# Sums over fields of x2 as three f32r matmuls in place of one fp32 matmul, on one core

## The reference

```python
x0 = xk = e                       # (512, 39, 16): rows, fields, depth
outs = []
for W in (f0, f1, f2):            # f0: (39*39, 128), f1 and f2: (39*128, 128)
    z = einsum('bfd,bgd->bfgd', x0, xk).reshape(b, f * g, d)
    cur = einsum('bpd,pm->bmd', z, W)
    outs.append(cur)
    xk = cur
z = sum(concatenate(outs, axis=1), axis=-1)          # over the depth d
h = maximum(concatenate([z, dense_ctx], axis=1) @ W_top1 + b_top1, 0)
h = maximum(h @ W_top2 + b_top2, 0)
y = h @ W_top3
```

## Time and profile before

| | |
|---|---|
| three runs, median | 807.4 us (805.65 to 807.54) |
| profiled execution | 809.94 us, span 808.1 us |
| TensorE matmul busy | 698.5 us, 86% |
| VectorE busy | 621.5 us, 77% |
| ScalarE busy | 488.2 us, 60% |
| GpSimd busy | 256.1 us, 32% |

### The profile page before, as it was taken

One profiled execution on the slowest core, in us unless ns is written; L12 is line 12 of the kernel. 1 busy time (PEld: TensorE's weight loads), 2 busy tenths in 40 slices (PEclk: granted clock), 3 DMA queues, 4 the chain that ended last, 5 costly groups with the idle time before them and its releaser, 6 DMA issues.

```text
span 808.1 us, 12253 instructions
## 1 busy us (share of the span) xinstructions
PE 698.5 (86%) x3327; PEld 498.2 (62%) x3327; DVE 621.5 (77%) x1409; ACT 488.2 (60%) x1659; POOL 256.1 (32%) x247
## 2 busy tenths in 40 slices
PE   0107899999999999999999979999999998999977
PEld 0002556666667776666666766666666686767757
DVE  1004698999999885799899865799899986799960
ACT  0002566776778663776677644676678564768851
POOL 6750026432661240812741330622651000211110
PEclk9999799999999999999999999999999999999989
DMA  3710202120212020020302020020202010020000
GB/s 82 282 41 1 72 10 61 25 70 13 66 22 72 10 64 22 5 80 2 85 4 80 2 66 21 4 75 8 77 12 72 9 57 25 3 78 1 2 0 1
DMA packets 23423, 33.96 MB, mean 42 GB/s; under 512 B 7816, under 2 KB 10616, under 8 KB 22967
## 3 DMA queue, kind: packets, MB, share of 16 engines
q1 hardware_dynamic: 18230, 31.84, 12.8%
q0 software_dynamic: 5120, 1.29, 1.9%
HBM read 9.13 MB, written 0.00 MB: 11 GB/s over the span
## 4 chain that ended last, share of the span: by engine, by line
PE 49%; DVE 25%; issue 11%; another core or an unknown queue 8%; ACT 5%; DVEq 1%; DMA 0%; SPq 0%; ACTq 0%
DVE sums L621 12%; PE x_ps L738 10%; PE v_ps L713 5%; PE v_ps L715 5%; PE v_ps L714 5%; PE s_ps L766 4%; PE a_ps L713 4%; PE a_ps L714 4%; PE a_ps L715 4%; DVE z_sb L594 3%; ACT scaled L419 3%; DVE scaled L564 2%; DVE sums L569 2%; PE s_ps L845 2%
## 5 line engine op out<-in xcount | busy, mean ns | idle before, releaser
L419 ACT ACTIVATE scaled<-a_ps,x0c 128x128 f32<-128x128 f32 x1216 | 352.2, 385 | 211.1 <-PE a_ps L715 187.6
L621 DVE SCALAR_TENSOR_TENSOR sums<-v_ps,x0c,sums 128x128 f32<-128x128 f32 x768 | 215.4, 341 | 59.2 <-PE v_ps L715 54.6
L363 POOL DMA_INDIRECT e_sb<-in_tables,ids_now x140 | 166.5, 1189 | 40.3 <-issue 38.1
L713 PE MATMUL v_ps<-w_hi,x_hi 128*128 128x512 f32 x320 | 175.8, 549 | 4.0 <-DVE w_lo L537 2.0
L379 POOL TENSOR_TENSOR diag_sb<-x0c,eye_sb 128x320 f32<-128x320 f32 x64 | 63.2, 988 | 360.3 <-PE s_ps L845 357.2
L738 PE MATMUL x_ps<-z_sb,w_sb 117*128 117x512 f32 (+1 forms) x210 | 115.0, 629 | 20.4 <-DVE z_sb L594 18.8
L715 PE MATMUL v_ps<-w_hi,x_lo 128*128 128x512 f32 x320 | 127.6, 399 | 0.0
L714 PE MATMUL v_ps<-w_lo,x_hi 128*128 128x512 f32 x320 | 127.5, 399 | 0.0
L713 PE MATMUL a_ps<-w_hi,x_hi 128*128 128x512 f32 (+1 forms) x320 | 124.4, 389 | 0.6 <-issue 0.5
L714 PE MATMUL a_ps<-w_lo,x_hi 128*128 128x512 f32 (+1 forms) x320 | 123.5, 386 | 0.0
L715 PE MATMUL a_ps<-w_hi,x_lo 128*128 128x512 f32 (+1 forms) x320 | 123.2, 385 | 0.0
(11 more groups left out here) (77 smaller groups left out, 659.4 us busy)
## 6 DMA issues: line engine op xcount, KB each, us to landing
b_sb<-a_sb SPq DMA_DIRECT2D x300, 78.0 KB
w_sb<-in_w SPq DMA_DIRECT2D x1, 2496.0 KB
e_sb<-in_tables,ids_now POOLq DMA_INDIRECT x140
s_sb<-in_w SPq DMA_DIRECT2D x2, 1024.0 KB
wt_sb<-in_wt SPq DMA_DIRECT2D x1, 768.0 KB
s_sb<-in_w SPq DMA_DIRECT2D x1, 512.0 KB
wt_sb<-in_wt SPq DMA_DIRECT2D x1, 512.0 KB
w_raw<-in_w0a SPq DMA_DIRECT2D x1, 409.5 KB
```

What stands on the lines that cost most here:

```text
L363: pool.indirect_dma_start(out=e_sb[0:rows, i, :], out_offset=None, in_=tables, in_offset=bass.IndirectOffsetOnAxis(ap=ids_now[0:rows, 0, i ...
L419: last = nc.scalar.activation(scaled[:, s % 2, to, j, :], bank[:, j * MAPS:(j + 1) * MAPS], ACT.Copy, scale=x0c[:, k % 4, s, lo + j:lo + j ...
L621: nc.vector.scalar_tensor_tensor(out=sums[:, s % 2, j, :], in0=v_ps[n % 2][:, j * MAPS:(j + 1) * MAPS], scalar=x0c[:, k % 4, s, lo + j:lo ...
L713: nc.tensor.matmul(to, high, w_high, start=True, stop=False)
```

## The change

S of a tile becomes three f32r matmuls: x2 high times diagonal high, x2 high times diagonal low, x2 low times diagonal high. The parts are made so:

- ScalarE rounds `x0c` to `x0c_hi`, once a chunk at step 18, and `x2t` to `x2_hi`, once a tile: tile 0 at step 11, tile 1 at step 16, tile 2 at step 1 of the next slot, tile 3 at step 6 of the next slot.
- GpSimd subtracts to get `x0c_lo`, once a chunk, and `x2_lo`, once a tile. It spreads both parts of x0, so a tile has two spreads in place of one.
- TensorE waits for `x2_lo_ready` where it waited for `x2t_ready`, and for two spreads in place of one.
- `z_first`, used at the start only, becomes a view of `scaled`, which makes room in SBUF.

VectorE's program keeps its instructions; one of its waits names `x2_lo_ready` in place of `s_done`.

```diff
--- before.py
+++ after.py
@@ -65,6 +65,12 @@
 
 
 S_AT = ((1, 4, 6, 9), (10, 12, 14, 17), (2, 6, 11, 17), (2, 6, 11, 17))
+
+
+X0C_HI_AT = 18
+
+
+X2_HI_AT = (11, 16, HALVES + 1, HALVES + 6)
 
 SPLIT_AT = (5, 8, 10, 13)
 X0_TURN_AT = (15, 17)
@@ -149,16 +155,23 @@
         a_sb = sb("a_sb", [3 * F0, COLS])
         b_sb = sb("b_sb", [3 * F0, SHIFT_BUFS, COLS])
         z0_sb = sb("z0_sb", [3 * F0, 2, COLS])
-        z_first = sb("z_first", [3 * F0, T0, COLS])
         w0_raw = sb("w0_raw", [3 * F0, 2, T0, MAPS])
         x1_hi = sb("x1_hi", [128, 2, COLS], f32r)
         x1_lo = sb("x1_lo", [128, 2, COLS], f32r)
 
         scaled = sb("scaled", [128, 2, SCALED, 4, MAPS])
         sums = sb("sums", [128, 2, 4, MAPS])
+
+        z_first = scaled.rearrange("p a g f m -> p (a g f m)")[0:3 * F0, 0:T0 * COLS]\
+            .rearrange("p (i c) -> p i c", c=COLS)
         pace = sb("pace", [128, 1, FH], i32)
         x2t = sb("x2t", [128, 2, SUBS, MAPS])
-        diag_sb = sb("diag_sb", [128, 2, SB, F0 + 1])
+        x2_hi = sb("x2_hi", [128, 2, SUBS, MAPS], f32r)
+        x2_lo = sb("x2_lo", [128, 2, SUBS, MAPS], f32r)
+        x0c_hi = sb("x0c_hi", [128, 2, SUBS, F0 + 1], f32r)
+        x0c_lo = sb("x0c_lo", [128, 2, SUBS, F0 + 1], f32r)
+        diag_hi = sb("diag_hi", [128, 2, SB, F0 + 1], f32r)
+        diag_lo = sb("diag_lo", [128, 2, SB, F0 + 1], f32r)
 
         s_sb = sb("s_sb", [128, 4 * FG, BT])
         out0 = sb("out0", [128, B])
@@ -221,6 +234,10 @@
         tail_step = sem("tail_step")
         x2t_ready = sem("x2t_ready")
 
+        x2_hi_ready = sem("x2_hi_ready")
+        x2_lo_ready = sem("x2_lo_ready")
+        x0c_hi_ready = sem("x0c_hi_ready")
+        x0c_lo_ready = sem("x0c_lo_ready")
         diag_ready = sem("diag_ready")
         s_done = sem("s_done")
         s_ready = sem("s_ready")
@@ -372,15 +389,31 @@
                     if h in diag_at and exists(t, k - 1):
                         s = diag_at.index(h)
                         before = tile_of(t, k - 1, s)
-                        pool.wait_ge(x0c_ready, 4 * t + k)
+                        if s == 0:
+                            pool.wait_ge(x0c_hi_ready, 4 * t + k)
+                            if not isinstance(t, int) or 4 * t + k - 1 >= 2:
+
+                                pool.wait_ge(diag_ready, 2 * tile_of(t, k - 2, 0))
+                            nc.gpsimd.tensor_tensor(x0c_lo[:, (k - 1) % 2, :, :], x0c[:, (k - 1) % 4, :, :],
+                                                    x0c_hi[:, (k - 1) % 2, :, :].bitcast(fp32),
+                                                    ALU.subtract).then_inc(x0c_lo_ready, 1)
                         if not isinstance(t, int) or before >= 2:
 
                             pool.wait_ge(s_done, before - 1)
+                        spread = mask.rearrange("p (b a) -> p b a", a=1).broadcast_to([128, SB, F0 + 1])
                         nc.gpsimd.tensor_tensor(
-                            diag_sb[:, s % 2, :, :],
-                            x0c[:, (k - 1) % 4, s:s + 1, :].broadcast_to([128, SB, F0 + 1]),
-                            mask.rearrange("p (b a) -> p b a", a=1).broadcast_to([128, SB, F0 + 1]),
-                            ALU.mult).then_inc(diag_ready, 1)
+                            diag_hi[:, s % 2, :, :],
+                            x0c_hi[:, (k - 1) % 2, s:s + 1, :].bitcast(fp32).broadcast_to([128, SB, F0 + 1]),
+                            spread, ALU.mult).then_inc(diag_ready, 1)
+                        pool.wait_ge(x0c_lo_ready, 4 * t + k)
+                        nc.gpsimd.tensor_tensor(
+                            diag_lo[:, s % 2, :, :],
+                            x0c_lo[:, (k - 1) % 2, s:s + 1, :].bitcast(fp32).broadcast_to([128, SB, F0 + 1]),
+                            spread, ALU.mult).then_inc(diag_ready, 1)
+                        pool.wait_ge(x2_hi_ready, before + 1)
+                        nc.gpsimd.tensor_tensor(x2_lo[:, (k - 1) % 2, s, :], x2t[:, (k - 1) % 2, s, :],
+                                                x2_hi[:, (k - 1) % 2, s, :].bitcast(fp32),
+                                                ALU.subtract).then_inc(x2_lo_ready, 1)
                     if k % 2 == 1 and h == GATHER_AT + 1 and exists(t, k + 3):
 
                         nc.gpsimd.tensor_tensor(pace[:, :, :], table_rows_sb[:, :, :], table_rows_sb[:, :, :],
@@ -435,11 +468,27 @@
                         act.wait_ge(x0c_done, 4 * t + k + 2)
                         if not isinstance(t, int) or 4 * t + k + 1 >= 4:
 
-                            act.wait_ge(diag_ready, tile_of(t, k - 2, 0))
+                            act.wait_ge(x0c_lo_ready, 4 * t + k - 2)
                             act.wait_ge(x2t_ready, tile_of(t, k - 2, 0))
                         nc.scalar.activation(x0c[:, (k + 1) % 4, :, 0:F0],
                                              turn_ps[:, 0:SUBS * F0].rearrange("p (s f) -> p s f", s=SUBS),
                                              ACT.Copy).then_inc(x0c_ready, 1)
+                    if h == X0C_HI_AT and exists(t, k):
+                        if not isinstance(t, int) or 4 * t + k >= 2:
+
+                            act.wait_ge(diag_ready, 2 * tile_of(t, k - 1, 0))
+                        nc.scalar.activation(x0c_hi[:, k % 2, :, :], x0c[:, k % 4, :, :],
+                                             ACT.Copy).then_inc(x0c_hi_ready, 1)
+                    for s in range(SUBS):
+                        of = k if X2_HI_AT[s] < HALVES else k - 1
+                        if h == X2_HI_AT[s] % HALVES and exists(t, of):
+                            before = tile_of(t, of, s)
+                            act.wait_ge(x2t_ready, before + 1)
+                            if not isinstance(t, int) or before >= 2 * SUBS:
+
+                                act.wait_ge(s_done, before - 2 * SUBS + 1)
+                            nc.scalar.activation(x2_hi[:, of % 2, s, :], x2t[:, of % 2, s, :],
+                                                 ACT.Copy).then_inc(x2_hi_ready, 1)
                     if h == X1_HI_AT and exists(t, k + 1):
                         act.wait_ge(x1_step, T0 * (4 * t + k + 2))
                         nc.scalar.activation(x1_hi[:, (k + 1) % 2, :], x1_ps[:, :], ACT.Copy).then_inc(x1_hi_ready, 1)
@@ -574,7 +623,7 @@
                     dve.wait_ge(tail_step, TAIL * tile + 5)
                     if not isinstance(t, int) or 4 * t + k >= 2:
 
-                        dve.wait_ge(s_done, tile - 2 * SUBS + 1)
+                        dve.wait_ge(x2_lo_ready, tile - 2 * SUBS + 1)
                     nc.vector.tensor_tensor(x2t[:, k % 2, s, :], acc[:, 0, :], acc[:, 1, :],
                                             ALU.add).then_inc(x2t_ready, 1)
 
@@ -838,13 +887,17 @@
                         if s == 0 and tile is not None and k == 1:
 
                             pe.wait_ge(out2_ready, tile + 1)
-                        pe.wait_ge(diag_ready, before + 1)
-                        pe.wait_ge(x2t_ready, before + 1)
+                        pe.wait_ge(diag_ready, 2 * before + 2)
+                        pe.wait_ge(x2_lo_ready, before + 1)
                         if not isinstance(t, int) or before > 0:
                             pe.wait_ge(s_ready, before)
-                        nc.tensor.matmul(s_ps[:, 0:SB * (F0 + 1)], x2t[:, (k - 1) % 2, s, :],
-                                         diag_sb[:, s % 2, :, :].rearrange("p b f -> p (b f)"),
-                                         start=True, stop=True).then_inc(s_done, 1)
+                        to = s_ps[:, 0:SB * (F0 + 1)]
+                        x0_high = diag_hi[:, s % 2, :, :].rearrange("p b f -> p (b f)")
+                        nc.tensor.matmul(to, x2_hi[:, (k - 1) % 2, s, :], x0_high, start=True, stop=False)
+                        nc.tensor.matmul(to, x2_hi[:, (k - 1) % 2, s, :],
+                                         diag_lo[:, s % 2, :, :].rearrange("p b f -> p (b f)"), start=False, stop=False)
+                        nc.tensor.matmul(to, x2_lo[:, (k - 1) % 2, s, :], x0_high,
+                                         start=False, stop=True).then_inc(s_done, 1)
 
             def first_pairs():
```

## The result

The changed kernel takes 839.3 us (median of four runs, 833.3 to 842.0), the kernel before, measured beside it, 806.9 us (805.7 to 807.5). The ratio is 1.039, with a 95% interval of 1.034 to 1.045: 32 us slower. The forecast was 819.0 us with a range of 803 to 833. Its direction was right, and its size was off by 20 us. Where the runs of a kernel spread, its ratio rests on those within 1.5% of its fastest. The profiled execution was the fastest of the four, 833.3 us, so that the profile holds 23.3 us of the loss (span 831.4 against 808.1 us).

The account below looks back on a forecast made before the run. VectorE was taken to bound ordinary slots, TensorE the dense ones. Terms -2.8 (TensorE), +9.5 (GpSimd on VectorE), +2.5 (ScalarE) and +2.4 (end) sum to +11.6 us on 807.4, so 819.0 us, range 803 to 833.

Parts of the forecast that it names:

- What bounds the kernel: VectorE sets the pace in the twelve ordinary slots, TensorE in the three slots where dense layers run.
- TensorE, -2.8 us: S matmuls: three f32r replace one fp32, saving 0.10 us a tile; 1.2 us in dense slots, 1.6 us in ordinary ones.
- What GpSimd does to VectorE, +9.5 us: Ordinary slots: GpSimd's added SBUF reads delay VectorE's two-SBUF-input operations; 7.9 us by rate, taken as 9.5 us.
- my upper bound of 25: Ordinary slots: each new GpSimd run costs VectorE one more full delay of 0.53 us, 48 tiles, 25 us.
- GpSimd's own added time: GpSimd: one more spread and a subtraction a tile, one subtraction a chunk; 111 us added in all.
- the rate of 0.095 us for each microsecond of spreads: VectorE delay per microsecond of GpSimd spreads, from L564 and L569; 10.5 us on 111 us, three quarters counted: 7.9 us.
- The bound of 0.53 us for each run: Upper bound for VectorE: each new GpSimd run costs one full delay as at 410.67, 25 us over 48 tiles.
- ScalarE, +2.5 us: Added roundings of x0c_hi and x2_hi, 24.3 us of work mostly hidden in waits; 1.8 plus 0.7 us reach the time.
- the term's two places: x0c_hi ahead of the a_sb copy, 1.8 us; x2_hi of tile 0 ahead of a dense layer's activations, 0.7 us.
- The end, +2.4 us: After the last x2t: longer chain +1.2 us, shorter matmuls -0.4 us; three more VectorE delays there, +1.6 us.
- every run of GpSimd costing a full operation: Rival: each GpSimd run costs VectorE 0.53 us a tile in ordinary slots, 25.4 us, time 834.9 us; chance 0.10.

Follow-up runs that it names:

- e8: Kernel before, with the fp32 S matmul made three f32r matmuls of the same two operands, nothing added on ScalarE or GpSimd: 802.3 us, ratio 0.995.
- e1: Kernel before, with a second spread and subtractions added on GpSimd alone, written to a spare buffer: 830.2 us, ratio 1.032.
- e14: Kernel before, with a second spread of the same size directly behind each spread, into a tensor nobody reads: 817.6 us, ratio 1.015.
- e9: Kernel before, with ScalarE's added roundings alone, at the steps of the change, into tensors nobody reads: 808.8 us, ratio 1.005.
- e13: Changed kernel with x0c_hi rounded at step 5 in place of 18, nothing else moved: 830.4 us, ratio 1.032 to the kernel before.
- e7: Changed kernel unaltered, measured again: 841.0 us, ratio 1.044 to the kernel before.

## Why the prediction was wrong

**What bounds the kernel.** Right. VectorE sets the pace of the ordinary slots, and what it lost there came out as time. The copy of x0c, once a chunk, before and after:

```profile
L440 ACT ACTIVATE x0c<-turn_ps x16: 316/320/332, 74.3 to 734.2; 128x156 f32<-128x156 f32 x16
```

```profile
L473 ACT ACTIVATE x0c<-turn_ps x16: 318/319/332, 74.7 to 755.0; 128x156 f32<-128x156 f32 x16
```

Between the first and the last lie 659.9 us before and 680.3 after, 20.4 of the 23.3 us. By the starts of the single copies, the twelve ordinary intervals grew by 2.2 us each, where I had said 0.5 to 1, and the three with dense layers, which I had said would not grow, fell by 2.1 us each; a boundary between two intervals may have moved too.

**TensorE, -2.8 us.** Right in mechanism and close in size: -4.0 us (e8). The step of 0.44 us is there. TensorE's timeline after:

```profile
338.45 0.31 PE L896 MATMUL s_ps<-diag_hi,x_hi 128*128 128x320 f32 x1
338.60 0.30 PE L897 MATMUL s_ps<-diag_lo,x_hi 128*128 128x320 f32 x1
338.74 0.31 PE L899 MATMUL s_ps<-diag_hi,x_lo 128*128 128x320 f32 x1
338.89 1.02 PE L787 MATMUL x_ps<-z_sb,w_sb 117*128 117x512 f32 x2
```

**What GpSimd does to VectorE, +9.5 us.** This is the step that failed: 25.7 us for it alone (e1, 20.5 to 30.7), 16 us more than I took, and at my upper bound of 25. It was the mis-sized term of a mechanism that is there. The means of L564 and L569 rose as foretold, to 785 and 739 ns, and VectorE's busy time by three times the 10 us that I named. GpSimd's own added time was close (97.5 us, 111 predicted). Two parts of the step were wrong.

First, the rate of 0.095 us for each microsecond of spreads. I read it from two lines and let the others "only add". All lines together had 10.5 us of delays for 63.2 us of spreads, 0.166; on 111 us, at three quarters, that is 13.8 us where mine gave 7.9. After the change z0 (13.3 us) and the 128x896 addition (6.9 us), which my rate left out, carry nearly half of the 43.4 us, and TensorE waits for z0.

Second, that rate came from a trace in which a spread nearly always stands alone, and I applied it to operations in a row. A lone spread delays VectorE's next operation by what is left of the spread, and can start beside the multiply-adds; the second and third of a row start when VectorE is past these. I wrote that two in a row make the second likelier to be in the way, and then added 1.6 us for it: e14 shows 12 us for the second alone. The count shows what the row adds. Waits through one operation grew about as GpSimd's operations did (23 to 72, where those went from 79 to 223), from 9.6 to 24.8 us. Waits through two to five are new, 15.7 us on ten operations, in e1 13.1 us on eleven. The bound of 0.53 us for each run had no place for them, since it took it that VectorE waits through no more than one. Mostly that holds; z0 at 258.54 lost 2.88 us at once. Why those ten were not let in, the runs do not tell.

**ScalarE, +2.5 us.** 4.3 us (e9, 2.0 to 6.5), over the term. Of it 1.0 us lies behind the last x2t, which the forecast has under the end: in e9's trace the 39 matmuls start 3.4 us after x2t, before 2.4. The 3.3 us left are within the bounds of the term's two places (3.6 and 1.2 us). x0c_hi is likely a good part of it: its move gave back 10 us in the changed kernel (e13 against e7), though there x0c_lo moves with it.

**The end, +2.4 us.** 3.7 us: from VectorE's last four multiply-adds to the 39 matmuls it is 9.47 us before (from 774.03) and 13.17 after (from 795.78). Of this 1.6 us lie ahead of the last x2t, as forecast for VectorE's delays there, and 2.1 behind it, where I had 0.8 (+1.2 and -0.4). The last x2t, and what follows it, after:

```profile
803.78 0.69 DVE L627 TENSOR_TENSOR x2t<-sums 128x128 f32<-128x128 f32 x1
804.29 0.50 POOL L414 TENSOR_TENSOR x_lo<-x2t,x_hi 128x128 fp32r<-128x128 f32 x1
804.51 0.31 ACT L490 ACTIVATE x_hi<-x2t 128x128 fp32r<-128x128 f32 x1 [0.18 <-DVE x2t L627]
...
804.89 0.60 PE L896 MATMUL s_ps<-diag_hi,x_hi 128*128 128x320 f32 x1 [1.31 <-POOL x_lo L414]
...
806.12 0.45 POOL L414 TENSOR_TENSOR x_lo<-x2t,x_hi 128x128 fp32r<-128x128 f32 x1
...
806.92 0.61 PE L896 MATMUL s_ps<-diag_hi,x_hi 128*128 128x320 f32 x1 [0.89 <-ACT s_sb L464]
...
808.95 0.77 PE L815 MATMUL s_ps<-s_sb,w_sb 128*128 128x128 f32 x2 [0.89 <-ACT s_sb L464]
```

The third copy of S releases the last matmuls, as I had said, but not because it stands behind x2_hi. It is late because the third S matmul (804.89) waited 1.31 us for x2_lo of its tile (804.29): from 795.75 to 806.57 GpSimd works without a break, and in the end it is GpSimd that sets the pace. I had counted it there beside VectorE and for the last x2_lo only. That the total came near the term, and within its bounds of 0 and 5, is partly luck.

**The sum.** The single runs give 25.7 + 4.3 - 4.0 = 26.0 us, and 27.1 with the 1.1 us of the end that e9 does not have. The change measures 32.4 us, and 35.7 in e7. The intervals of e1 and of the change are 5 us to each side, so that the first gap (5.3 us) may be noise, the second (8.6 us) less likely so. If it is real, two things in the traces bear on it. TensorE's new waits for GpSimd (8.4 us for diag_lo and 4.7 us for x2_lo) are no candidate: all of them lie behind 795, in the end counted above. But VectorE's delays are 43.4 us, against 30.9 in e1, and z0 has 13.3 of them, against 4.1. In the changed kernel x0c_lo waits for ScalarE's x0c_hi, which moves GpSimd's run. With x0c_hi at step 5 (e13) z0's delays are 7.1 us and the kernel is 10 us faster. That it is this was argued from these numbers and not isolated.

**The rivals.** The one that I gave 0.10, every run of GpSimd costing a full operation, had its 834.9 us nearest. Its price, 0.53 us a run, is near the mean (32.9 us of added delays on 64 runs, 0.51), and that is partly luck: no run costs just this. Most delays are shorter (0.34 us in the mean for the 72), and the ten long ones (1.6 us in the mean) make up for it.
